# Readback of expert rows: the last four columns summed by TensorE through diagonal gate matrices, with their loads issued second

## The chip, the cores and the metric

One core of one Trainium2 chip (trn2). The metric is the device time of one execution of the whole program in microseconds, here the median of three runs.

## The reference, cut to what matters

The program computes a small two-layer network on 8 images (64 patches each) with 8 texts (128 tokens each), 1536 tokens of 192 features in f32. Layer 0 has a recurrent mixer and a mixture of 8 experts, layer 1 a linear attention and a second mixture of 8 experts. The change lies where the first mixture's result is added to the residual and the attention of layer 1 begins:

```python
# layer 0, experts: each token takes its two best experts
for e in range(8):
    y = gelu(flat_x @ w1[e] + b1[e]) @ w2[e] + b2[e]
    out = out + y * gates[:, e:e + 1]
h = h + out
# layer 1, attention
x = layernorm(h)
qkv = einsum('bnc,dc->bnd', x, qkv_w)
q_, k_ = relu(q) + SCALE, relu(k) + SCALE
kv = einsum('bnhe,bnhd->bhed', k_, v)
out = einsum('bnhe,bhed->bnhd', q_, kv) * z
h = h + out @ proj_w.T + proj_b
```

## The kernel before, in words

The residual h is kept in SBUF as 12 columns of 128 tokens by 192 features (h[:, j, :], j = 0 to 11; columns 0-3 hold the patches, 4-11 one text each). xn and a1 are buffers of the same shape.

Order of the work is written out by hand: each engine has one instruction stream (a block per engine), and semaphores join them.

*The experts of layer 0* work on 28 tiles of 128 token slots. For each tile TensorE writes the products of the second weights, VectorE copies them out of PSUM (L1697) and GpSimd scatters the rows to a DRAM buffer, expert_rows, with an indirect DMA (L797): one row for each token and choice, 1536 rows for the first choice and 1536 for the second. ScalarE copies weights and does the Gelu.

*The readback.* load_acc (lines 560 to 569) waits for all scatters and then loads the rows back in token order: SyncE's queue brings those of the first choice into xn, ScalarE's queue those of the second into a1. Each does so in four loads by the groups of ACC = ((0, 2), (2, 4), (4, 8), (8, 12)): columns 0-1, 2-3, 4-7 and 8-11, in this order, each with a semaphore acc_ld[g] for both queues together. A load of two columns has 192 KB, one of four 384 KB. Behind them SyncE's queue issues 32 loads of the layer-1 expert weights (L631 to L634), and then one copy.

*The sums*, on VectorE (L1754 to L1763): for each group of columns it waits for the group's two loads, then adds gate times row to h, one instruction for each column and choice (L1759, all columns of the first choice, then all of the second). ln_start (L1270, L1273) makes mean and variance of each column of the group. ScalarE takes the root (ln_std, L883), VectorE makes 1/root and the shift (ln_end, L1289 and L1290, two small operations); ScalarE normalizes into xn (ln_norm, L896, one instruction a column). ln_end of a group stands between the first and the second half of the next group's sums; that of the last group stands behind the first k_evac.

*Layer-1 projections.* TensorE transposes pairs of normalized columns (t_pair(3, q), L1985), ScalarE copies them out (xt3_evac, L1181). kv_mms(g) makes keys and values of four columns (L2383, L2389), q_mms(g) the queries (L2415, L2420). VectorE applies relu to keys (k_evac, L1771) and queries (q_evac, L1779), ScalarE copies the values (v_evac, L1190, L1191), behind k_evac. q_mms(0) waits for rwg_ready, since its banks 6 and 7 were used before by filler products and by small products that VectorE copies out (L1751 to L1753). Then come the attention's sums (L2437, L2443, L2459, L2464), the transposes (L2471) and the output projection (L2494).

*Fillers.* keep_busy(n, bank) (L1931) issues n products of 512 columns whose result nobody reads; 18 of them stand before the first transposes of layer 1. Such products also stand ahead of the routing of both layers.

*Table loads.* ScalarE loads a table when its function changes to another set: once after load_acc, for the root (at L883).

Of the kernel before, what the change touches and what calls it, by code (L numbers as in the profile page):

```python
# [30 lines left out]
ACT = mybir.ActivationFunctionType  # L31
# [71 lines left out]
def build(nc, x, out):  # L103
    ctx = ExitStack()
    with ctx:
# [217 lines left out]
        qT = carve(reg2, NK * NTOK)[0:KC, :].rearrange("p (g t) -> p g t", g=NK)  # L323
        kb = carve(reg2, NJ * D).rearrange("p (j n) -> p j n", j=NJ)
# [62 lines left out]
        rank_mm = sem("rank_mm"); oneB_ready = sem("oneB_ready"); lg1_ready = sem("lg1_ready"); one_ready = sem("one_ready")  # L387
# [174 lines left out]
        def load_acc(eng, p):  # L562

            wait_scatters(eng, 0)
            buf = (xn, a1)[p]
            rows = tok_rows(ybuf, p * NTOK)
            for g, ab in enumerate(ACC):
                js = slice(*ab)
                eng.dma_start(buf[:, js, :], rows[:, js, :]).then_inc(acc_ld[g], 16)
# [292 lines left out]
        def _(act):  # L862
# [313 lines left out]

            load_acc(act, 1)
# [17 lines left out]
            for q in range(2):  # L1195
                ln_std(3, q)
                ln_norm(3, q, h)
                xt3_evac(q)
            for g in range(1, 3):
                ln_std(3, g + 1)  # L1200
                ln_norm(3, g + 1, h)
                v_evac(g - 1)
                xt3_evac(2 * g)
                xt3_evac(2 * g + 1)
# [41 lines left out]
        def _(dve):  # L1246
# [507 lines left out]
            for g, ab in enumerate(ACC):  # L1754

                dve.wait_ge(acc_ld[g], 16 * 2)
                for k, y in ((0, xn), (1, a1)):
                    for j in range(*ab):
                        ins = V.scalar_tensor_tensor(out=h[:, j, :], in0=y[:, j, :], scalar=gate[:, k, j:j + 1],  # L1759
                                                     in1=h[:, j, :], op0=ALU.mult, op1=ALU.add)  # L1760
                    link(ins)
                    if g and k == 0:
                        ln_end(3, g - 1)  # L1763
                ln_start(3, g, h)

# [120 lines left out]
            for g in range(2):  # L1886
                k_evac(g)
                if g == 0:
                    ln_end(3, 3)
                q_evac(g)  # L1890
# [33 lines left out]
        def _(pe):  # L1924
# [444 lines left out]
            keep_busy(18, 6)  # L2369
# [31 lines left out]
            def q_mms(g):  # L2401


                if g:
                    pe.wait_ge(q_ev, 2 * g)
                else:

                    pe.wait_ge(rwg_ready, 1)
# [226 lines left out]
```

## Time and profile before

| | |
|---|---|
| median of 3 runs | 430.27 us |
| lowest, highest | 426.57, 430.79 us |
| the profiled execution: device time | 428.35 us |
| its span, first to last instruction | 426.6 us |
| granted TensorE clock, mean over the span | 0.958 |

The profiled execution is one of its own beside the three; 1.75 us of its time lie outside the span. Times in the rows are us from the start of the span. PE is TensorE, DVE VectorE, ACT ScalarE, POOL GpSimd, SP SyncE; a q behind the name is an engine's sequencer or queue. Lines such as L1759 are lines of the kernel before.

### The profile page before, as it was taken

What the parts mean: (1) busy time and instruction counts of PE and PEld (TensorE: products, weight loads), DVE (VectorE), ACT (ScalarE), POOL (GpSimd) and SP (SyncE); (2) the same over time, 40 slices, a digit from 0 to 9 for tenths busy, and PEclk for the clock granted to TensorE, in tenths of its full rate; (3) what the DMA queues carried; (4) which work ended last, traced back from release to release, by engine and by line L of the source; (5) the groups of instructions that cost most, each with busy time, mean ns of one, the idle gap of its engine ahead of it and who ended that gap; (6) DMA issues with size and microseconds to landing.
All of it is one profiled execution on the core that took longest, in us unless ns stands there. A gap on an engine that the chain in (4) does not pass through costs nothing.

```text
span 426.6 us, 11079 instructions
## 1 busy us (share of the span) xinstructions
PE 398.4 (93%) x3904; PEld 299.8 (70%) x3913; DVE 279.8 (66%) x1298; ACT 230.3 (54%) x424; POOL 221.3 (52%) x233
## 2 busy tenths in 40 slices
PE   8999999998769999999788999978999999999993
PEld 5653756666434666666535689538999999999993
DVE  6689999889974444444495368876565656556551
ACT  1287963560675566665146115575565656666550
POOL 5323779798036677774400003444566565566524
PEclk9899689999988999999699999969999999999999
DMA  8609300010142222221499996522243333343323
GB/s 243 112 13 263 73 0 2 2 37 1 34 141 70 60 78 77 84 77 48 131 273 229 233 230 183 171 44 72 46 66 47 67 51 61 47 67 55 47 21 35
DMA packets 38921, 38.29 MB, mean 90 GB/s; under 512 B 7667, under 2 KB 36129, under 8 KB 38853
## 3 DMA queue, kind: packets, MB, share of 16 engines
q1 hardware_dynamic: 27937, 22.85, 22.0%
q0 software_dynamic: 9024, 13.44, 16.4%
q10 hardware_dynamic: 1906, 1.30, 1.0%
q8 instruction: 32, 0.52, 0.5%
q14 instruction: 22, 0.18, 0.1%
HBM read 27.73 MB, written 10.53 MB: 90 GB/s over the span
## 4 chain that ended last, share of the span: by engine, by line
DMA 23%; PE 14%; DVE 5%; issue 5%; ACT 2%; POOL 1%; POOLq 1%; DVEq 0%; ACTq 0%
DMA out<-a,idx 21%; PE bank L2494 2%; PE bank L2095 2%; DVE h L1759 2%; PE bank L2383 1%; PE bank L2140 1%; PE bank L2464 1%; POOL out L809 1%; PE bank L1931 1%; DMA a<-expert_rows 1%; PE bank L2415 1%; DVE st L1270 1%; PE bank L2389 1%; ACT reg L1073 1%; PE bank L2437 1%
## 5 line engine op out<-in xcount | busy, mean ns | idle before, releaser
L809 POOL DMA_INDIRECT out<-a,idx x31 | 50.4, 1626 | 46.6 <-DMA out<-a,idx 32.8
L789 POOL DMA_INDIRECT reg<-xn_rows,idxs x59 | 57.7, 978 | 27.1 <-issue 14.5
L2095 PE MATMUL bank<-reg,xT 64*128 64x128 f32 x1116 | 69.2, 275 | 0.5 <-DVE reg L1671 0.5
L2140 PE MATMUL bank<-reg 64*128 64x192 f32 x744 | 65.6, 323 | 0.0
L2095 PEld LDWEIGHTS bank<-reg,xT 64*128 64x128 f32 x1116 | 65.2, 188 | 0.6 <-DVE reg L1671 0.6
L2140 PEld LDWEIGHTS bank<-reg 64*128 64x128 f32 x744 | 60.0, 187 | 0.0
L1105 ACT ACTIVATE reg<-reg 128x1152 f32 x31 | 36.1, 1163 | 33.8 <-PE bank L2140 33.8
L1700 DVE TENSOR_SCALAR a<-bank,gs 128x192 f32<-128x192 f32 x31 | 13.0, 418 | 53.3 <-PE bank L2140 53.3
L1931 PE MATMUL bank<-con 128*128 128x512 bf16 x154 | 42.4, 429 | 1.5 <-issue 1.0
L797 POOL DMA_INDIRECT expert_rows<-a,idx x28 | 27.6, 985 | 15.4 <-DVE a L1697 9.3
L1697 DVE COPY a<-bank 128x192 f32<-128x192 f32 x28 | 10.0, 358 | 36.2 <-PE bank L2133 36.2
L2078 PE MATMUL bank<-reg,xTs 96*64 (+1 forms) x112 | 33.2, 419 | 0.5 <-DVE xTs L1661 0.5
L2081 PE MATMUL bank<-xT,xTs 96*64 96x288 f32 (+1 forms) x112 | 33.2, 419 | 0.0
L1671 DVE TENSOR_SCALAR reg<-bank,gb 128x128 f32<-128x128 f32 x93 | 32.3, 402 | 0.0
L1931 PEld LDWEIGHTS bank<-con 128*128 128x128 bf16 x163 | 17.2, 110 | 21.1 <-issue 8.3
L2130 PE MATMUL bank<-reg 96*64 x168 | 31.9, 326 | 0.0
L2133 PE MATMUL bank<-xT,reg 96*64 96x192 f32 x168 | 31.9, 326 | 0.0
L1124 ACT ACTIVATE xT<-reg 97x576 f32 x28 | 19.1, 682 | 23.5 <-PE bank L2133 23.5
L838 POOL TENSOR_SCALAR onep<-rs 128x3 f32<-128x3 f32 x4 | 0.9, 230 | 53.4 <-DVE nm L1282 53.4
L2130 PEld LDWEIGHTS bank<-reg 96*64 96x64 f32 x168 | 22.7, 136 | 7.5
L1088 ACT ACTIVATE reg<-bank 128x384 f32<-128x384 f32 x31 | 15.2, 491 | 16.2 <-PE bank L2095 16.2
L2133 PEld LDWEIGHTS bank<-xT,reg 96*64 96x64 f32 x168 | 22.7, 136 | 0.0
(373 smaller groups left out, 878.5 us busy)
## 6 DMA issues: line engine op xcount, KB each, us to landing
reg<-in_w2b SPq DMA_DIRECT2D x8, 576.0 KB, 10.8
reg<-in_w1b SPq DMA_DIRECT2D x8, 288.0 KB, 10.5
reg<-in_w1a SPq DMA_DIRECT2D x8, 216.0 KB
reg<-in_w2a SPq DMA_DIRECT2D x8, 216.0 KB
reg<-in_w1b SPq DMA_DIRECT2D x8, 192.0 KB, 8.4
xn_rows<-xn SPq DMA_DIRECT2D x3, 384.0 KB, 2.6
reg<-in_patchT SPq DMA_DIRECT2D x2, 512.0 KB, 5.5
reg<-xn_rows,idxs POOLq DMA_INDIRECT x59
```

The costliest lines, as they stand in the source:

```text
L789: pool.indirect_dma_start(xs[:, i % RING, 0:(D, D2)[l]], None, xd[l], bass.IndirectOffsetOnAxis(ap=idxs[:, i:i + 1], axis=0)).then_inc(xs_ ...
L797: pool.indirect_dma_start(ybuf, bass.IndirectOffsetOnAxis(ap=idx2[:, i:i + 1], axis=0), ys[:, i % YRING, :], None).then_inc(scat[i % YRING ...
L809: pool.indirect_dma_start(out, bass.IndirectOffsetOnAxis(ap=idx2[:, i:i + 1], axis=0), ys[:, i % YRING, :], None, compute_op=ALU.add).then ...
L1105: nc.scalar.activation(w2r[:, p, :], w2b.rearrange("p e c n -> p (e c n)")[:, bass.ds(e * W2R, W2R)], ACT.Copy).then_inc(w2r_act, 1)
L1671: ins = V.tensor_scalar(dst[:, k], src[:, :, 64 * k:64 * k + 64], gb2[:, 0, k:k + 1], gb2[:, 1, k:k + 1], ALU.mult, ALU.add)
L1931: MM(bank[bk][:, :], con[:, 0:P // 2].bitcast(BF16), con[:, 0:2 * P].bitcast(BF16), start=True, stop=True)
L2078: MM(bank[2 + p][0:GR, 0:hid], xTs[0:r, p, k, 0:GR], w1v[0:r, bass.ds(e * (NK * hid) + k * hid, hid)], start=(k == 0), stop=(k == NK - 1))
L2081: ins = MM(bank[2 + p][GR:P, 0:hid], xTs[0:r, p, k, GR:P], w1u[0:r, i % 3, k * hid:(k + 1) * hid], start=(k == 0), stop=(k == NK - 1))
L2095: ins = MM(bank[2 + 2 * p + a][:, c * P:(c + 1) * P], w1r[rs, p, col:col + hc], xT64[rs, p, k, :], start=(c == 0 and k == 0), stop=(c == n ...
L2130: MM(bank[6 + p][0:GR, 0:D], hTs[0:r, p, c * P:c * P + GR], w2v[0:r, bass.ds(e * (nhc * D) + c * D, D)], start=(c == 0), stop=(c == nhc - 1))
L2133: ins = MM(bank[6 + p][GR:P, 0:D], hTs[0:r, p, c * P + GR:(c + 1) * P], w2u[0:r, i % 2, c * D:(c + 1) * D], start=(c == 0), stop=(c == nhc ...
L2140: ins = MM(bank[Y_BANKS[i == NT - 1][a]][:, 0:D], hT2[rs, p, c * P:(c + 1) * P], w2r[rs, p, c * D:(c + 1) * D], start=(c == 0), stop=(c == ...
```

## The change

What it does:
- load_acc issues its four loads in the order 0, 3, 1, 2: columns 0-1, 8-11, 2-3, 4-7.
- ScalarE, after the last products of the layer-0 experts and ahead of load_acc on its queue, scales the identity by each of the gates of columns 8-11: dg, eight 128x128 diagonal matrices (two choices, four columns), in the space of the layer-0 weights.
- TensorE, after 16 instead of 18 filler products, waits for the loads of columns 8-11, for dg and for rwg_ready, and sums in PSUM, for each of the four columns, identity times h, first diagonal times the first choice's rows, and second diagonal times the second's. That is 12 products of 192 columns, in banks 6 and 7, two columns of tokens in each.
- ScalarE copies the two banks to h (two copies of 128x384), behind the transposed copy of the second pair and ahead of the norm of columns 4-7. q_mms(0) waits for these copies.
- VectorE has no sums of columns 8-11 any more; it waits for the copies and makes mean and variance. ln_end of groups 2 and 3 stands behind that, ahead of the first k_evac. ln_end of groups 0 and 1 moves to the middle of the next group's first half.
- ScalarE's two last roots (groups 2 and 3) stand together ahead of both norms.

```diff
--- before.py
+++ after.py
@@ -321,6 +321,7 @@
         w2a = carve(reg2, NE * (HID0 // HC0) * D)[0:KC + 1, :].rearrange("p (e c n) -> p e c n", e=NE, n=D)
         o = 0
         qT = carve(reg2, NK * NTOK)[0:KC, :].rearrange("p (g t) -> p g t", g=NK)
+        dg = reg2[:, 0:2 * 4 * P].rearrange("p (k j n) -> p k j n", k=TOPK, j=4)
         kb = carve(reg2, NJ * D).rearrange("p (j n) -> p j n", j=NJ)
         vb = carve(reg2, NJ * NK * KV).rearrange("p (j n) -> p j n", n=KV)
         vb4 = vb.rearrange("p (j a) n -> p j a n", a=NK)
@@ -384,7 +385,7 @@
         back_mm = sem("back_mm")
         xd_written = sem("xd_written")
         sums_mm = sem("sums_mm"); rsum_ready = sem("rsum_ready"); h_added = sem("h_added"); lg_mm = sem("lg_mm"); ex_in = sem("ex_in"); ex_out = sem("ex_out"); msk_ready = sem("msk_ready")
-        rank_mm = sem("rank_mm"); oneB_ready = sem("oneB_ready"); lg1_ready = sem("lg1_ready"); one_ready = sem("one_ready")
+        rank_mm = sem("rank_mm"); oneB_ready = sem("oneB_ready"); dg_ready = sem("dg_ready"); add_mm = sem("add_mm"); add_ev = sem("add_ev"); lg1_ready = sem("lg1_ready"); one_ready = sem("one_ready")
         gate_ready = sem("gate_ready")
         slot_ready = sem("slot_ready"); oneP_ready = sem("oneP_ready"); oneS_ready = sem("oneS_ready")
         inv_mm = sem("inv_mm")
@@ -564,8 +565,8 @@
             wait_scatters(eng, 0)
             buf = (xn, a1)[p]
             rows = tok_rows(ybuf, p * NTOK)
-            for g, ab in enumerate(ACC):
-                js = slice(*ab)
+            for g in (0, 3, 1, 2):
+                js = slice(*ACC[g])
                 eng.dma_start(buf[:, js, :], rows[:, js, :]).then_inc(acc_ld[g], 16)
 
 
@@ -1174,6 +1175,11 @@
             experts(0, ACT.Gelu, HID0)
 
 
+            act.wait_ge(g2_mm, NT0)
+            for k in range(TOPK):
+                for n, j in enumerate(range(*ACC[3])):
+                    nc.scalar.activation(dg[:, k, n, :], con[:, C_ID:C_ID + P], ACT.Identity,
+                                         scale=gate[:, k, j:j + 1]).then_inc(dg_ready, 1)
             load_acc(act, 1)
             def xt3_evac(q):
 
@@ -1196,8 +1202,14 @@
                 ln_std(3, q)
                 ln_norm(3, q, h)
                 xt3_evac(q)
+            act.wait_ge(add_mm, 1)
+            for b in range(2):
+                nc.scalar.activation(h[:, 8 + 2 * b:10 + 2 * b, :],
+                                     bank[6 + b][:, 0:2 * D].rearrange("p (j n) -> p j n", j=2),
+                                     ACT.Copy).then_inc(add_ev, 1)
+            ln_std(3, 2)
+            ln_std(3, 3)
             for g in range(1, 3):
-                ln_std(3, g + 1)
                 ln_norm(3, g + 1, h)
                 v_evac(g - 1)
                 xt3_evac(2 * g)
@@ -1751,17 +1763,21 @@
             V.tensor_copy(rsum[:, :, :], bank[7][:, 0:2 * NE].rearrange("p (v e) -> p v e", v=2))
             V.tensor_copy(prw[0:KC, :, D:DL], bank[7][0:KC, 3 * NE:5 * NE].rearrange("p (m e) -> p m e", m=NK))
             V.tensor_copy(prw[KC:KC + 1, 1, D:DL], bank[7][KC:KC + 1, 2 * NE:3 * NE]).then_inc(rwg_ready, 1)
-            for g, ab in enumerate(ACC):
+            for g, ab in enumerate(ACC[0:3]):
 
                 dve.wait_ge(acc_ld[g], 16 * 2)
                 for k, y in ((0, xn), (1, a1)):
-                    for j in range(*ab):
+                    for n, j in enumerate(range(*ab)):
                         ins = V.scalar_tensor_tensor(out=h[:, j, :], in0=y[:, j, :], scalar=gate[:, k, j:j + 1],
                                                      in1=h[:, j, :], op0=ALU.mult, op1=ALU.add)
+                        if g and k == 0 and n == (ab[1] - ab[0]) // 2 - 1:
+                            ln_end(3, g - 1)
                     link(ins)
-                    if g and k == 0:
-                        ln_end(3, g - 1)
                 ln_start(3, g, h)
+            dve.wait_ge(add_ev, 2)
+            ln_start(3, 3, h)
+            ln_end(3, 2)
+            ln_end(3, 3)
 
             def k_evac(g):
 
@@ -1885,8 +1901,6 @@
 
             for g in range(2):
                 k_evac(g)
-                if g == 0:
-                    ln_end(3, 3)
                 q_evac(g)
             state(0)
             k_evac(2)
@@ -2366,7 +2380,17 @@
                              start=(k == 0), stop=(k == NK - 1))
             ins.then_inc(bias_mm, 1)
 
-            keep_busy(18, 6)
+            keep_busy(16, 6)
+            pe.wait_ge(acc_ld[3], 16 * 2)
+            pe.wait_ge(dg_ready, TOPK * 4)
+            pe.wait_ge(rwg_ready, 1)
+            for n, j in enumerate(range(*ACC[3])):
+
+                rows_j = bank[6 + n // 2][:, (n % 2) * D:(n % 2 + 1) * D]
+                MM(rows_j, ident, h[:, j, :], start=(n % 2 == 0), stop=False)
+                MM(rows_j, dg[:, 0, n, :], xn[:, j, :], start=False, stop=False)
+                ins = MM(rows_j, dg[:, 1, n, :], a1[:, j, :], start=False, stop=(n % 2 == 1))
+            ins.then_inc(add_mm, 1)
             t_pair(3, 0)
 
             def kv_mms(g):
@@ -2405,7 +2429,7 @@
                     pe.wait_ge(q_ev, 2 * g)
                 else:
 
-                    pe.wait_ge(rwg_ready, 1)
+                    pe.wait_ge(add_ev, 2)
 
                 def half(m):
                     return slice(m * 2 * P, (m + 1) * 2 * P)
```

## Rows read from the trace of the kernel before

**Rows 1.** Part 1 of the page: busy us, share of the span, instructions, by engine.
```profile
PE 398.4 (93%) x3904; PEld 299.8 (70%) x3913; DVE 279.8 (66%) x1298; ACT 230.3 (54%) x424; POOL 221.3 (52%) x233
```

**Rows 2.** Chain that ended last, 195 to 262 us: start us, us, what.
```profile
205.30 2.35 DMA expert_rows<-a,idx
...
207.87 4.00 DMA a<-expert_rows
...
214.36 0.64 DVE h L1759 x2
...
216.98 0.79 DVE h L1759 x3
...
218.67 1.33 DVE h L1759 x4
...
221.57 0.39 DVE h L1759 x2
...
224.62 1.15 DVE st L1270 x4
...
226.20 0.57 DVE reg L1771
...
228.35 1.55 PE bank L2383 x4
...
252.13 2.24 PE bank L2494 x12
```

**Rows 3.** Third and fourth load of a queue: issues (start, us), us to landing.
```profile
210.19 1.13 ACTq L569 DMA_DIRECT2D a<-expert_rows  x2
...
a<-expert_rows ACTq DMA_DIRECT2D x1, 384.0 KB, 5.2
xn<-expert_rows SPq DMA_DIRECT2D x1, 384.0 KB, 5.9
...
210.76 0.56 ACTq L569 DMA_DIRECT2D a<-expert_rows  x1
...
xn<-expert_rows SPq DMA_DIRECT2D x1, 384.0 KB, 8.0
a<-expert_rows ACTq DMA_DIRECT2D x1, 384.0 KB, 10.2
```

**Rows 4.** Timeline around the readback, and L1073: start us, us, engine line, [idle before].
```profile
204.00 0.32 PE L2133 MATMUL bank<-xT,reg 97*64 97x192 f32 x1
...
210.55 5.09 PE L1931 MATMUL bank<-con 128*128 128x512 bf16 x17 [0.23 <-issue]
...
211.35 1.28 ACT L883 ACT_TABLE_LOAD   x1 [8.61 <-issue]
...
218.70 0.98 ACT L896 ACTIVATE xn<-h,nmr,rstd 128x192 f32<-128x192 f32 x2 [0.99 <-DVE nmr L1290]
...
223.30 1.86 ACT L896 ACTIVATE xn<-h,nmr,rstd 128x192 f32<-128x192 f32 x4 [1.40 <-DVE nmr L1290]
...
223.45 1.97 PE L2415 MATMUL bank<-reg 128*96 128x256 f32 x8
...
226.39 0.87 PE L1985 MATMUL bank<-con,xn 128*128 128x128 f32 x6
...
227.71 0.88 ACT L1181 ACTIVATE reg<-bank 128x384 f32<-128x384 f32 x2
...
278.37 1.57 ACT L1073 ACTIVATE reg<-iotab,slf 128x128 f16<-128x128 f16 x5 [3.38 <-DVE slf L1591]
```

**Rows 5.** TensorE after two gaps: timeline, and windows (us, busy, PEclk, DMA).
```profile
117.61 0.46 PE L2011 MATMUL bank<-msk,con 128*128 128x96 f32 x2 [2.02 <-DVE msk L1546]
...
206.31 1.02 PE L2360 MATMUL bank<-rwg,con 96*128 96x8 f32 x4 [1.98 <-DVE reg L1746]
...
206.30:213.10 6.80, 6.56 (x26) 0.50 0.56 151
...
117.60:121.00 3.40, 3.39 (x19) 1.00 0.86 257
```


## The prediction

> **What bounds the kernel now.** I read the page first: TensorE is busy for 398.4 of 426.6 us and no other engine for more than 280 [rows 1]. That is a mean over stages, so the next view was the chain of waits around the readback, the stage that the change touches. In it the reader is to see three limits one after the other [rows 2]. The last scatter of expert rows lands at 205.30 + 2.35 = 207.65. Then a load decides: issued at 207.87, landed 4.00 later, at 211.87, for the first two columns. From there VectorE decides: the sums of columns 2-3 start at 214.36, of 4-7 at 216.98, of 8-11 at 221.57, and the relu of the keys, L1771, at 226.20. TensorE takes over at 228.35 with the second group of key and value products, and from there to past 250 the chain is TensorE alone. So the figure that carries to the end is the 228.35: what moves it moves the end by as much, and what doesn't is worth nothing.
>
> The third view was the landings, since VectorE looks bound by its own work only as long as its data are there first [rows 3]. The third load of each queue (columns 4-7) starts at 210.19 and takes 5.2 on ScalarE's queue and 5.9 on SyncE's, which started within 0.02 us of it: 216.1 for both. The fourth (8-11) starts near 210.7 and takes 8.0 on SyncE's queue, 218.7, and 10.2 on ScalarE's, 210.76 + 10.2 = 220.96. VectorE asked for them at 216.98 and 221.57: 0.9 and 0.6 us of slack. The loads are nearly as late as the sums. That is the number of this case.
>
> **The change, part by part.** The sum goes against the profiled execution: span 426.6, 428.35 us in all, 1.9 below the median of the three runs (430.27). What I find as a difference I add to the median.
>
> *Sums taken off VectorE.* Eight multiply-adds go. Four take 1.33 us [rows 2], so 2.7 us. The statistics of columns 8-11 stay (224.62 to 226.20, 1.58 us). The two small operations of ln_end(3,3), which ran between two evacuations, now come before them. Their price: 226.20 - 221.57 = 4.63 is eight multiply-adds (2.67), the statistics (1.58) and one ln_end, so 0.37 for that. If nothing is waited for, VectorE is 2.3 us sooner at L1771.
>
> *Order of the loads.* The bytes and the number of issues are the same, the order is columns 0-1, 8-11, 2-3, 4-7 on both queues, with the 32 weight loads behind them on SyncE's queue as before. I take the landings by columns moved: 2 by 211.87, 8 by 216.1, 12 by 220.96 (an estimate from [rows 2, 3], as nothing is issued more or sooner). So columns 8-11 land at some 214.7 (six columns, in line between the first two), 2-3 at 216.1, and 4-7 at 220.96. VectorE is free for 2-3 at 214.36 and waits 1.7 us. Its work on them is 216.98 - 214.36 = 2.62, so it asks for 4-7 at 218.7 and waits 2.2 us more. Bounds for this last landing, which I call L: 216.98 or sooner (no wait, below) and 220.96 plus what ScalarE adds, next. SyncE's 218.7 lies between them. I take 220.96, since the sum needs both queues and ScalarE's was the later.
>
> *Diagonal matrices on ScalarE.* Eight scalings of 128x128 wait for the last product of the experts (204.00 + 0.32) and stand ahead of load_acc on that queue. ScalarE was idle from 211.35 - 8.61 = 202.74 [rows 4], so the loads are what they could delay. Five operations of the same width with a pointer operand took 1.57, 0.31 each; four of 192 columns took 1.86, 0.47 each [rows 4]. Eight are 2.5 to 3.7 us, ending at 206.9 to 208.1 against the scatter's 207.65. I take the 0.31 of equal width: hidden, 0.7 us to spare. The other end costs 0.45, and a table load, 1.28 [rows 4], would cost up to 1.7 in all; I keep that as the top of the range of L.
>
> *Products on TensorE.* Two of 18 filler products go (17 recorded ones take 5.09 us to 215.64, 0.3 each [rows 4]), so the filler ends near 215.1. Then it waits for the load of 8-11 (214.7), for dg_ready and rwg_ready (both long there). Twelve products of 96x200 took 2.24 [rows 2]; twelve of 192 columns over all 128 rows I take at 2.2. Bounds: twelve times half of a 392-column product (1.55 / 4 / 2) is 2.3, and one alone without overlap is no more than a whole such product, 4.7 for twelve. Queued behind them on TensorE are the transposes of columns 0-1. These need their norms: landing 216.1, one sum (0.33), ln_end (0.37), two norms (0.98), 217.9. The products end at 217.3: hidden, by the wait for columns 2-3; at 4.7 they would end at 219.8 and hold the first transposes 1.9 us, but these are then still ahead of the next ones at L + 2.1. Without that wait (norms at 216.1) they would stand 1.3 us in the way of the first transposes, but not of VectorE.
>
> *Copies out of PSUM on ScalarE.* Two of 128x384, 0.49 each by its like at 227.71 (0.88 for two overlapped) [rows 4]. They come after the norm of 2-3 and its copy, L + 3.2, and end at L + 4.2. VectorE reaches them after its group of four columns, 221.57 - 216.98 = 4.59, at L + 4.6: hidden with 0.4 us to spare. The new wait of the query products for them costs nothing either, as those start at L + 5.8 (next).
>
> *Scalings amid the sums.* ln_end after half of the first half of a group instead of after all of it: 0.33 us sooner for a pair, 0.67 for four. It is used above. It gains nothing where a load is late.
>
> **The sum from L to the hand-over.** Sums and statistics of 4-7: 4.59. Statistics of 8-11: 1.58. ln_end(3,2): 0.37. Four norms on ScalarE: 1.86 and 0.04 to start. They used to be done at 225.2 (223.30 + 1.86) [rows 4], before L1771; now they come after it and in front of the value copies. That eats what VectorE gave. Value copies: 227.71 - (226.20 + 0.57) = 0.94. First xT3 copy to the first product of the second group: 228.35 - 227.71 = 0.64. In all L + 10.0. TensorE's own way there: two sums and ln_end 1.04, two norms 1.02, then as before 223.45 - (218.70 + 0.98) = 3.77 to the query products and 226.39 - 223.45 = 2.94 to the next transposes: L + 8.8, later than the norms (L + 8.4) but within what the value copies take.
> With L = 220.96 the hand-over is at 231.0 against 228.35: +2.6 us. It is even at L = 218.3. **Forecast: 430.27 + 2.6 = 432.9 us**, some 431.0 for an execution like the profiled one. All behind runs on TensorE, shifted.
>
> **Rivals.** *A, the loads land ahead of need; not slower.* With columns 2-3 by 214.36 and 4-7 by 216.98 the hand-over is 216.98 + 10.0 = 227.0, -1.4: 428.9. One place decides, L, and the point is 218.3. For it: the third issue starts only at 210.19, 2.3 after the first; if the queues ran short of work behind that, a second load of four columns in place of two would fill the gap. SyncE's own last landing was 218.7, only 0.4 over. Against it: the same bytes have to pass before L, and ScalarE's queue needed to 220.96.
> *B, TensorE's clock falls in the new wait.* The first transposes start at 217.9, take some 0.44 (half of the six at 226.39), their copy 0.5, the first key products 1.55: TensorE then idles from 220.4 to L + 2.1 = 223.1, 2.7 us. Before, it idled 1.98 us up to 206.31, and the granted clock from there to 213.10 was 0.50, the 1.2 GHz level [rows 5]. But it also idled 2.02 us up to 117.61, and the clock behind that stayed at 1.00, the 2.4 GHz level [rows 5]: such a gap can bring a fall, and need not. From 223.1 some 6.6 us of products lie ahead of the hand-over. With a fall there that lasts as long as that one, 6.8 us, 3.4 are done by 230.1 and the rest by 233.4, the hand-over comes near 234.1, +5.7: 436.0. The Trainium skill (TensorE: Matmul & The Clock Gate, "HAM oscillation") says that a kernel whose bursts of products are parted by waits on DMA is throttled again and again and begins its bursts cold. By that rule B is the outcome; the gap before 117.61 speaks against its certainty.
> *C, ScalarE's scalings hold up its loads.* With 0.47 each or a table load L moves by 0.45 to 1.7: +3.1 to +4.3, 433.4 to 434.6. One engine's queue decides, and the table load would be seen before 207.
> *D, nothing reaches the hand-over:* L near 218.3, loads and sums even, 430.3.
>
> **How the numbers follow.** Forecast 0.46, A 0.16, B 0.19, C 0.06, D 0.13. The three runs shown lie 4.2 us apart, so a change under 1% (4.3 us) is about what this kernel can't tell from none. Faster by over 1% needs under 426.0, three times A's gain: 0.06. Slower needs over 434.6, which is B, the upper part of C and the forecast in a bad draw: 0.24. The rest is 0.70. The range: down to 427.5, A with a lucky draw of runs; up to 436.5, B.
>
> **What would show it.** Right: VectorE idle before the first L1759 of column 2 (some 1.7 us) and of column 4 (some 2), both put down to a load; the second L2383 group near 231; L896 for 4-7 after L1771; the twelve products done before the transposes of 0-1; no table load before the readback. If the clock row between 220 and 230 shows 0.50, it is B. If VectorE waits for nothing there, or the fourth load lands before 218.3, the forecast is wrong and A or D holds. If the scalings end after 207.7, it is C. A change of the end that isn't the change of the hand-over would mean that a stage behind it, not this one, moved.

## The result, and the profile after

| | before | changed |
|---|---|---|
| median (20 runs each) | 427.62 us | 429.74 us |
| lowest, highest | 425.54, 430.79 | 426.71, 432.35 |
| ratio, 95% interval | | 1.0056 (1.0037 to 1.0076) |
| profiled execution: time, span | 428.35, 426.6 us | 426.71, 424.9 us |

By the ratio the change costs 0.56%, 2.4 us (1.6 to 3.2); the two medians lie 2.1 us apart. The forecast was 2.6 us slower. Its absolute 432.9 lay 3.2 us too high, and 2.65 of these are the median of three on which it stood (430.27, against 427.62 for twenty).

The profiled execution of the changed kernel is the fastest of its twenty, and its span is shorter than that of the profile before: its readback alone starts 2.83 us sooner in the span. So absolute times of the two profiles can't be compared. I compare from t0, the start of the first load of the readback (before 207.87, ScalarE's queue), to the hand-over, the first product of the second key group, which is L2383 before and L2407 after.

The chain of waits of the changed kernel, 204 to 232 us (start us, us, what), where every piece from the filler on is one of TensorE's or a copy that it waits for:

```profile
206.20 6.28 PE bank L1945 x16
212.48 0.33 PE bank L2390 x2
...
216.06 0.33 PE bank L2392 x2
216.38 0.34 PE bank L1999 x3
...
216.75 0.50 ACT reg L1187
...
226.12 0.50 ACT reg L1187
...
226.75 1.55 PE bank L2407 x4
```

Its t0 is 205.04 and the hand-over 226.75: t0 + 21.71, against 228.35 - 207.87 = 20.48 in [rows 2]. That is 1.2 us later. Where VectorE's sums stood in the chain before, there now stands TensorE: sixteen fillers, twelve products (L2390 to L2392), the first transposes, ScalarE's copy of them (216.75), TensorE's own work up to the next transposes, and their copy (226.12).

The products by form, from the groups of instructions between 203 and 230 us (count, busy us, mean ns of one record, idle before):

```profile
L2390 PE MATMUL bank<-h,con 128*128 128x192 f32 x8 | 2.0, 326 | 0.0
L2391 PE MATMUL bank<-xn,reg 128*128 128x192 f32 x8 | 2.0, 326 | 0.0
L2392 PE MATMUL bank<-a,reg 128*128 128x192 f32 x8 | 2.0, 326 | 0.0
```

They are twelve matrix products in the code and 24 records in the trace: each f32 product leaves two, of 0.326 us each and overlapping by half. The chain above has a product ("x2") every 0.33 us: 12 x 0.33 = 3.9 us, from 212.48 to 216.38.

The landings, from the DMA view in narrow windows (SyncE's third issue begins at 206.31, the fourth of ScalarE's at 206.95), answering [rows 3]:

```profile
xn<-expert_rows SPq DMA_DIRECT2D x1, 384.0 KB, 5.0
a<-expert_rows ACTq DMA_DIRECT2D x1, 384.0 KB, 5.5
...
a<-expert_rows ACTq DMA_DIRECT2D x1, 192.0 KB, 5.6
xn<-expert_rows SPq DMA_DIRECT2D x1, 192.0 KB, 6.1
...
xn<-expert_rows SPq DMA_DIRECT2D x1, 384.0 KB, 8.1
a<-expert_rows ACTq DMA_DIRECT2D x1, 384.0 KB, 9.1
```

Behind t0: columns 8-11 by 6.0, 2-3 by 7.4, 4-7 by 11.0. The last landing of the readback came at t0 + 13.1 before.

The timeline of the same stretch (start us, us, engine, line, idle before and its releaser), which answers [rows 4]; L1771 is the L1759 of before, L1787 its L1771, L897 its L896, L1187 its L1181, and the L1181 of this view is the line of ScalarE's scalings:

```profile
203.62 0.38 ACT L1181 ACTIVATE reg<-con,gate 128x128 f32<-128x128 f32 x1
...
207.47 1.28 ACT L884 ACT_TABLE_LOAD   x1 [3.47 <-issue]
...
212.43 0.42 DVE L1771 SCALAR_TENSOR_TENSOR h<-xn,gate,h 128x192 f32<-128x192 f32 x1 [1.43 <-DMA xn<-expert_rows]
...
216.04 0.75 DVE L1771 SCALAR_TENSOR_TENSOR h<-xn,gate,h 128x192 f32<-128x192 f32 x2 [0.87 <-DMA a<-expert_rows]
...
216.75 0.49 ACT L1187 ACTIVATE reg<-bank 128x384 f32<-128x384 f32 x1 [2.61 <-PE bank L1999]
...
217.46 0.17 DVE L1301 RECIPROCAL rstd<-std 128x2 f32<-128x2 f32 x1 [0.67 <-ACT std L884]
...
223.71 1.02 DVE L1787 TENSOR_SCALAR reg<-bank 128x384 f32<-128x384 f32 x2
```

VectorE waits for columns 2-3 (1.43) and for 4-7 (0.87), and a third time, 0.67 us for the root of columns 2-3 at 217.46. The mean and variance for that root were there at 215.17, but ScalarE stood in its own order at the copy of the first transposes (2.61 idle at 216.75), and these came late because TensorE was at its products. No table load comes before the scalings; the only one of the readback follows the loads, as before.

### The profile page after: what moved, and what is told of

It is laid out like the page before. It is cut to its first block, busy times and chain, and to the rows that moved or that the text cites. A ratio compares the mean times of both kernels' runs of the same rounds, so it can differ in the third digit from the quotient of the medians.

```text
span 424.9 us, 11132 instructions
## 1 busy us (share of the span) xinstructions
PE 400.2 (94%) x3935; PEld 300.3 (71%) x3935; DVE 277.1 (65%) x1290; ACT 233.4 (55%) x434; POOL 221.4 (52%) x233
## 4 chain that ended last, share of the span: by engine, by line
PE 49%; DMA 25%; DVE 10%; ACT 6%; issue 6%; POOL 3%; POOLq 1%; DVEq 0%; ACTq 0%
DMA out<-a,idx 24%; PE bank L2092 7%; PE bank L2144 6%; PE bank L1945 3%; PE bank L2201 3%; PE bank L2407 2%; PE bank L2518 2%; DVE bank L1421 2%; PE bank L2271 2%; PE bank L2067 2%; ACT reg L1074 1%; PE bank L1960 1%; PE bank L2439 1%; PE bank L1953 1%; PE bank L2313 1%
## 5 line engine op out<-in xcount | busy, mean ns | idle before, releaser
L790 POOL DMA_INDIRECT reg<-xn_rows,idxs x59 | 57.7, 978 | 26.5 <-issue 14.3
L1945 PE MATMUL bank<-con 128*128 128x512 bf16 x161 | 43.6, 426 | 0.0
L798 POOL DMA_INDIRECT expert_rows<-a,idx x28 | 27.6, 986 | 14.3 <-DVE a L1709 8.2
## 6 DMA issues: line engine op xcount, KB each, us to landing
reg<-in_w1b SPq DMA_DIRECT2D x8, 288.0 KB, 11.3
```

Of the source, the lines that this page charges most:

```text
L790: pool.indirect_dma_start(xs[:, i % RING, 0:(D, D2)[l]], None, xd[l], bass.IndirectOffsetOnAxis(ap=idxs[:, i:i + 1], axis=0)).then_inc(xs_ ...
L798: pool.indirect_dma_start(ybuf, bass.IndirectOffsetOnAxis(ap=idx2[:, i:i + 1], axis=0), ys[:, i % YRING, :], None).then_inc(scat[i % YRING ...
L1945: MM(bank[bk][:, :], con[:, 0:P // 2].bitcast(BF16), con[:, 0:2 * P].bitcast(BF16), start=True, stop=True)
```

## The experiments

One table first, since all profiles are read by the same figures: us behind t0, from the timeline, chain and DMA view of each profile. L, here and below, is the landing of columns 4-7. Landings are good to 0.1 us. "Tail" is from the hand-over to the end of the span.

| profile | columns 2-3 | 4-7 | last landing | products end | hand-over | tail |
|---|---|---|---|---|---|---|
| before | 5.8 | 8.3 | 13.1 | | 20.48 | 198.2 |
| changed | 7.4 | 11.0 | 11.0 | 11.3 | 21.71 | 198.2 |
| changed_again | 8.8 | 12.8 | 12.8 | 11.8 | 22.81 | 197.9 |
| loads_alone | 9.4 | 13.5 | 13.5 | | 25.03 | 199.6 |
| products_alone | 6.0 | 8.4 | 12.8 | 11.2 | 22.42 | 199.7 |
| norm_first | 9.0 | 12.9 | 12.9 | 12.0 | 22.84 | 199.6 |
| fewer_fillers | 10.1 | 14.6 | 14.6 | 14.3 | 24.67 | 198.1 |
| hold_weights | 9.0 | 11.0 | 11.0 | 12.0 | 22.35 | 199.6 |
| hold_weights_before | 6.1 | 8.5 | 10.7 | | 20.19 | 198.2 |
| keys_first | 6.0 | 9.6 | 13.7 | | 20.39 | 199.4 |
| keys_first_again | 5.7 | 9.6 | 13.4 | | 20.32 | 198.1 |
| keys_first_held | 6.4 | 8.7 | 11.0 | | 19.77 | 199.4 |
| products_sooner | 7.9 | 10.1 | 10.1 | 10.5 | 21.64 | 198.1 |

### loads_alone: only the order of the loads

```diff
-            for g, ab in enumerate(ACC):
-                js = slice(*ab)
+            for g in (0, 3, 1, 2):
+                js = slice(*ACC[g])
```

> The kernel before with only the order of the readback's loads changed (0, 3, 1, 2); VectorE still sums all four groups in the order 0, 1, 2, 3. t0 is the start of the first load. Theory Loads (the late landing of columns 4-7 decides): VectorE waits for columns 2-3 and again for 4-7, which land 11 to 13 us behind t0, and reaches the first relu of the keys 9.2 us behind that landing, at t0 + 20.2 to 22.3 against t0 + 18.3 before: 1.9 to 4.0 us slower. Theory Array (what the change costs is TensorE's products, the loads are nearly free): under 0.7 us slower.

431.66 us against 427.26: ratio 1.0088 (1.0054 to 1.0122), 3.8 us. Its chain, 204 to 235 us, and below it two lines of VectorE's timeline:

```profile
209.48 11.03 DMA a<-expert_rows
...
229.88 0.57 DVE reg L1771
```

```profile
216.45 0.75 DVE L1759 SCALAR_TENSOR_TENSOR h<-xn,gate,h 128x192 f32<-128x192 f32 x2 [3.43 <-DMA xn<-expert_rows]
...
220.54 1.41 DVE L1759 SCALAR_TENSOR_TENSOR h<-xn,gate,h 128x192 f32<-128x192 f32 x4 [1.35 <-DMA a<-expert_rows]
```

The load that begins at 209.48 needs 11.03 us; VectorE idles 3.43 us for columns 2-3 and 1.35 for 4-7, then runs without a gap to L1771 at t0 + 22.88. The order of the loads alone costs VectorE 4.6 us. L1771 comes at L + 9.4, about as expected (9.2), and later than t0 + 22.3 because L was 13.5 and not 11 to 13. Array's "under 0.7 us" lies outside the interval (2.3 to 5.2 us) and is out for this part.

One thing more happened here. TensorE stood 3.86 us in front of its first transposes, and its granted clock was 0.50, the 1.2 GHz level, from 219.3 to 222.7:

```profile
219.40:222.70 3.30, 2.91 (x4) 1.17 (x4) 2.09 (x8) 0.85 (x3) 0.00 (x0) 0.50 1.11 233
```

That is what rival B describes. It did not reach the hand-over, since the chain from the landing on is VectorE's.

### products_alone: only the scalings and the products

```diff
+            act.wait_ge(g2_mm, NT0)
+            for k in range(TOPK):
+                for n, j in enumerate(range(*ACC[3])):
+                    nc.scalar.activation(dg[:, k, n, :], con[:, C_ID:C_ID + P], ACT.Identity,
+                                         scale=gate[:, k, j:j + 1]).then_inc(dg_ready, 1)
             load_acc(act, 1)
...
-            keep_busy(18, 6)
+            keep_busy(16, 6)
+            pe.wait_ge(dg_ready, TOPK * 4)
+            pe.wait_ge(rwg_ready, 1)
+            for n in range(4):
+                rows_j = bank[6 + n // 2][:, (n % 2) * D:(n % 2 + 1) * D]
+                MM(rows_j, ident, con[:, 0:D], start=(n % 2 == 0), stop=False)
+                MM(rows_j, dg[:, 0, n, :], con[:, 0:D], start=False, stop=False)
+                MM(rows_j, dg[:, 1, n, :], con[:, 0:D], start=False, stop=(n % 2 == 1))
```

> The kernel before with only the eight scalings on ScalarE ahead of its loads, 16 instead of 18 fillers, and twelve products of the change's shapes behind them, on constant data that is there already; nobody reads them, and VectorE still does all sums. Theory Loads: the products are hidden by the wait for the norms or nearly, 0 to 0.3 us slower. Theory Array: they take 3.9 us (0.325 for each of 24 records), the first transposes come 2.5 us later, ScalarE's copy behind them holds the root of columns 2-3, and VectorE waits for it in front of its second half of columns 4-7: about 2 us slower.

429.84 us against 427.26: ratio 1.0059 (1.0036 to 1.0083), 2.5 us. Array holds here, with its size (about 2 us expected, 1.5 to 3.5 measured). The timeline of 210 to 222 us:

```profile
216.18 0.49 PE L1991 MATMUL bank<-con,xn 128*128 128x128 f32 x3
216.70 0.49 ACT L1187 ACTIVATE reg<-bank 128x384 f32<-128x384 f32 x1 [3.34 <-PE bank L1991]
...
217.48 0.17 DVE L1295 RECIPROCAL rstd<-std 128x2 f32<-128x2 f32 x1 [2.25 <-ACT std L884]
```

Nothing reads these products. Still VectorE stands 2.25 us between the halves of columns 4-7, for a root; ScalarE, which takes it, stood 3.34 us for the first transposes; and they stood behind the products. My forecast had called this "hidden".

### fewer_fillers: 12 instead of 16 ahead of the products

```diff
-            keep_busy(16, 6)
+            keep_busy(12, 6)
```

> The changed kernel with 12 instead of 16 fillers ahead of the products. Theory Loads: TensorE is not what is waited for, no change against the changed kernel, so 2.1 us slower than before. Theory Array: the products start up to 1.5 us sooner, as soon as columns 8-11 are there, the first transposes too, and the hand-over to TensorE comes 0.7 us sooner than in the changed kernel: 1.2 to 1.5 us slower than before. A fall of the clock behind the shorter run of fillers could take it back.

430.61 us against 427.26: ratio 1.0090 (1.0056 to 1.0124), 3.8 us. Neither number came. The profile shows two things at once. Its loads landed later than in any other profile (columns 8-11 at t0 + 8.4, 4-7 at t0 + 14.6), which the fillers don't explain; and the clock fell in the middle of the products. Its chain, and a row of the windows view (us, busy by engine, PEclk, DMA):

```profile
207.74 7.91 DMA a<-expert_rows
...
216.61 0.33 PE bank L2392 x2
216.93 0.63 PE bank L2390 x2
217.56 0.64 PE bank L2391 x2
...
231.91 1.55 PE bank L2407 x4
```

```profile
216.80:220.20 3.40, 3.40 (x12) 3.40 (x11) 2.60 (x10) 0.98 (x2) 0.00 (x0) 0.50 1.10 247
```

With fewer fillers TensorE stood 1.9 us in front of the products, for the load of columns 8-11, and from 216.81 on they ran at 0.64 instead of 0.33 a product, at the 1.2 GHz level, for 3.4 us. That is rival B again, and it cost some 1.7 us of products. The chain here goes by these products and not by L: they end at t0 + 14.3, and the hand-over is that + 10.4. But L, at 14.6, would have put it at the same place (L + 10.06), so the fall of the clock cost this execution next to nothing. As a test of Array it is inconclusive.

### norm_first: norms and first relu ahead of the last statistics

```diff
-            dve.wait_ge(add_ev, 2)
-            ln_start(3, 3, h)
             ln_end(3, 2)
-            ln_end(3, 3)
...
             for g in range(2):
                 k_evac(g)
+                if g == 0:
+                    dve.wait_ge(add_ev, 2)
+                    ln_start(3, 3, h)
+                    ln_end(3, 3)
                 q_evac(g)
```

(ScalarE takes the two last roots each ahead of its own norm.)

> The changed kernel with VectorE's order behind the sums of columns 4-7 turned: ln_end of these, the first relu of the keys, and only then the wait for the copies and the statistics of columns 8-11; ScalarE takes the two last roots apart again. Theory Loads (the chain behind the landing L of columns 4-7 is VectorE's and ScalarE's, L + 10.7 as measured): it shortens to about L + 9, 1.1 us or more off the changed kernel's time, so 1 us slower than before or less. Theory Array (TensorE's own way, L + 9.5 to the end of the query products, is just behind): 0.2 to 0.4 us off the changed kernel's time.

430.90 us against 427.26: ratio 1.0097 (1.0062 to 1.0133), 4.1 us, no gain at all; both numbers expected are missed. Its timeline, 216 to 229 us:

```profile
223.53 1.86 ACT L897 ACTIVATE xn<-h,nmr,rstd 128x192 f32<-128x192 f32 x4 [0.44 <-DVE nmr L1301]
...
227.37 0.87 ACT L1187 ACTIVATE reg<-bank 128x384 f32<-128x384 f32 x2 [1.08 <-PE bank L1999]
```

The norms of 4-7 start at L + 5.5 here; in changed_again they start at L + 6.5. Yet the hand-over is L + 10.0 in both (22.84 - 12.86, 22.81 - 12.84): ScalarE then stands 1.08 us at 227.37 for TensorE's transposes. So the chain behind L is TensorE's own from the second transposes on, L + 2.1. Why the time came out even above the changed kernel's (its interval overlaps that one's only from 1.0062 to 1.0076) stays open; the hand-over of this one profile is that of changed_again.

### changed_again: the changed kernel once more

> The changed kernel once more, for a second profile of it: its first had the last landing 11.0 us behind the start of the loads (t0), while the kernel before and four others had 12.8 to 14.6. Theory Loads: the last landing L is 12.8 or later here and the hand-over to TensorE (second group of key products) comes at L + 10 to 10.8, that is t0 + 23 to 24, against 20.5 before and 21.7 in the first profile; the time is 2 to 3 us above before. Theory Array: the hand-over does not follow L but stays at t0 + 21.7.

430.05 us against 427.92: ratio 1.0051 (1.0028 to 1.0074). The chain of this second profile:

```profile
208.82 10.40 DMA a<-expert_rows
...
219.24 0.75 DVE h L1771 x2
...
220.30 0.99 ACT xn L897 x2
...
221.33 0.55 PE bank L1999 x3
...
228.05 0.49 PE bank L1999 x3
...
229.19 1.55 PE bank L2407 x4
```

Here the fourth load decides. It lands at 219.22, t0 + 12.84; two sums, ln_end and two norms follow, and TensorE takes over at L + 2.1. The hand-over is 229.19 = L + 9.97. The forecast's sum from L, 10.0, is met to 0.03. Loads holds: the hand-over followed L, by 0.2 us less than the t0 + 23 at the lower end of what was expected.

### hold_weights: the weight loads only behind the readback

```diff
             load_acc(sp, 0)
+            sp.wait_ge(acc_ld[2], 16 * 2)
```

> The changed kernel with one wait more: SyncE issues the 32 loads of layer-1 weights only when columns 4-7 have landed, so the readback has the DMA engines to itself. Theory Loads (their landing decides, and the weights slow it): L comes down to 9.5 to 10.5 us behind t0, the hand-over to some t0 + 21, and the time to 0.5 us above before or less. Theory Array (the products and what queues behind them decide): the hand-over stays where the products put it, t0 + 21.7, the time 1.2 us or more above before.

428.72 us against 427.92: ratio 1.0022 (0.9999 to 1.0045). That lies between the two theories (0.5 us or less, 1.2 or more). By the middle values more than half of the cost is gone; the interval overlaps those of changed and changed_again, so it is likely and not certain. Its chain:

```profile
205.15 7.27 DMA a<-expert_rows
...
212.47 0.59 PE bank L2391 x2
...
216.64 0.34 PE bank L2000 x3
...
227.01 1.55 PE bank L2408 x4
```

L is down to 11.0 and no longer in the chain; what is there is the second load (columns 8-11, 7.27 us), then the products to 216.6, and TensorE to the hand-over at 227.01. So there are two limits, and the later one counts: landing of 4-7 + 10.0, and end of the products + 10.4 (21.71 - 11.35 in the first profile of the changed kernel, 22.35 - 11.98 here). In the kernel before neither stood as late. The hand-over of this one profile, 22.35, is 1.9 above before, while the time is only 0.9 us above: columns 8-11 landed as late as 7.8 here (6.0 and 7.6 in the two profiles of the changed kernel), and one profile doesn't give the mean of the runs.

### hold_weights_before: the same wait in the kernel before

The edit is that of hold_weights with acc_ld[3].

> The kernel before with the same wait, for columns 8-11, ahead of the weight loads. Theory Loads: before the change the loads were 0.6 us ahead of VectorE's sums, so an earlier landing gives nothing, 0 to -0.4 us. If the weights come too late for the experts of layer 1, it is slower; they had some 20 us to spare.

427.10 us against 427.92: ratio 0.9992 (0.9964 to 1.0019), as expected no difference. The last landing is 2.4 us sooner and nobody waits for it.

### keys_first, keys_first_again: the first relu ahead of the last sums

The sums of a group became a function, and in the kernel before:

```diff
-            for g, ab in enumerate(ACC):
...
+            for g in range(3):
+                group(g)
+            ln_end(3, 2)
...
                 k_evac(g)
                 if g == 0:
+                    group(3)
                     ln_end(3, 3)
```

> The kernel before, sums all on VectorE and loads in the old order, with the first relu of the keys (and ln_end of columns 4-7) ahead of the sums of columns 8-11 instead of behind them. By the view that VectorE's chain sets the hand-over, and TensorE's own way ends at t0 + 19.5 (transposes of columns 4-5 at 18.5 + 0.44, copy 0.5): the hand-over comes 0.8 to 1.0 us sooner, and the time is 0.8 us below before. If something behind it (norms of columns 8-11, needed for the transposes at t0 + 25) is late instead, no gain.

426.90 us against 427.92: ratio 0.9976 (0.9950 to 1.0002), 1.0 us below by the middle value.

> keys_first once more, since its interval (0.9950 to 1.0002) just held no change and keys_first_held showed none. If the hand-over, 0.1 us sooner in the profile of keys_first and 0.7 in that of keys_first_held, reaches the end: 0.5 to 0.9 us below before, a ratio of 0.998 to 0.999. Rival: the clock's low stretch at the routing of layer 1, 6.8 us in one piece in some profiles and 10.2 in one or two pieces in others, gives it back at random: a ratio within 0.1% of 1.

427.58 us against 427.18: ratio 1.0013 (0.9987 to 1.0039). Between them they show no gain that could be told from none. In both profiles VectorE waited for columns 4-7 (0.9 and 1.1 us), so the hand-over was at 20.39 and 20.32: what VectorE gave, the loads took.

### keys_first_held: both together

> keys_first and hold_weights_before together: sums all on VectorE in the old order of loads, the first relu of the keys ahead of the sums of columns 8-11, and the weight loads issued only when the readback has landed. In the profile of keys_first columns 4-7 landed 9.6 us behind t0 and VectorE waited 0.9 us for them. Theory (max of two limits: landing of 4-7, and TensorE's own way): without the weights they land by t0 + 8.4, the hand-over comes at t0 + 19.3 to 19.6 against 20.5 before, and the time is 0.9 us below before. Rival: the gain given back behind the hand-over, no difference.

427.74 us against 427.60: ratio 0.9994 (0.9969 to 1.0018). The hand-over came at t0 + 19.77, 0.7 sooner than before and 0.2 later than expected. The time doesn't show it, and can't exclude it either: 0.7 us is 0.17%, inside the interval. In the one profile the tail, 199.4 instead of 198.2 (last section), takes more than that back. No version of this study beats the kernel before by more than the noise.

### loads_alone_held: the order alone, weights held

The edits of loads_alone and hold_weights.

> loads_alone with the weight loads issued only when columns 4-7 have landed. Theory Loads: hand-over = L + 11.5 as in loads_alone (25.0 - 13.5), and L comes down to 11 or to VectorE's own need (landing of columns 2-3, near 9, + 2.6): hand-over at t0 + 22.5 to 23.2 instead of 25.0, the time 2 us above before instead of 3.8. Rival: the weights' share of the DMA engines is not what makes the last landing late: 25, 3.8 us.

431.46 us against 427.60: ratio 1.0082 (1.0053 to 1.0111), 3.5 us, by the time the rival's number. The landing did come sooner, t0 + 11.3. The profile is of an execution of 442.75 us, far above the others. A piece of its chain and a row of the windows view show why its hand-over, t0 + 24.20, says little:

```profile
230.22 2.98 PE bank L2384 x4
```

```profile
227.60:234.20 6.60, 4.89 (x12) 2.78 (x14) 6.39 (x27) 2.97 (x7) 0.00 (x0) 0.50 0.64 157
```

TensorE stood 5.35 us in front of its first transposes, the clock was at the 1.2 GHz level from 227.5 to 234.3, and two key products took 2.98 us instead of 1.58. So here, unlike in loads_alone, TensorE's own way set the hand-over. VectorE, whose four sums take 1.40 us here as in loads_alone, reached the first relu (L1772) at 238.48, t0 + 21.28, 1.6 us sooner than in loads_alone. The loads did give VectorE what the theory says; that the time of the other executions shows no more than 0.3 us of it stays open. A fall of the clock in most of them would explain it, and no profile shows that.

### products_sooner: columns 8-11 loaded first, weights held, 12 fillers

```diff
-            for g in (0, 3, 1, 2):
+            for g in (3, 0, 1, 2):
...
-            keep_busy(16, 6)
+            keep_busy(12, 6)
```

> hold_weights with columns 8-11 loaded first of all and 12 instead of 16 fillers. There the hand-over was the end of the products (t0 + 12.0) + 10.4. Theory (products' end + 10.4, or landing of 4-7 + 10.0, the later): the products start at t0 + 6 and end at t0 + 10, the hand-over comes at t0 + 21 to 21.5, 1 us sooner than in hold_weights, if the landing of 4-7 stays at 11 or sooner; time no more than 0.5 us above before. Rival: the shorter run of fillers or the longer wait lets the clock fall and takes it back; 2 us above before.

429.43 us against 427.60: ratio 1.0059 (1.0032 to 1.0086). The products ran from t0 + 6.4 to 10.5, but the hand-over was 21.64, only 0.7 sooner than in hold_weights, and 0.8 behind the products' end + 10.4. Its chain:

```profile
205.39 6.03 DMA a<-expert_rows
...
211.44 0.76 DVE h L1772 x2
...
217.62 0.99 ACT xn L898 x2
...
218.66 0.55 PE bank L2000 x3
```

Columns 0-1 now land at t0 + 6.5. From there VectorE works without a gap to the norms of columns 2-3, and the second transposes wait for these. That is a third limit, VectorE's sums from the first landing on, which the theory of two limits left out. The time, 2.5 us above before, is that of the rival, though the clock did not fall behind the products in this profile; the tail was of the short kind. What the time is made of beyond the hand-over's 1.2 us is open.

## Why the prediction was right or wrong

**The direction: right. The mechanism: right in one of the two profiles of the changed kernel.** VectorE idles for columns 2-3 and for 4-7 in both (1.43 and 0.87; 2.53 and 1.29). loads_alone shows the reorder by itself: 3.8 us. What VectorE lost by it is larger than the 2.7 us that it was relieved of. But only changed_again has the fourth load in its chain. In the first profile there is no load in it, and the hand-over is set by the products, which the forecast had put at nothing ("hidden").

**The difference: 2.6 forecast, 2.4 measured (1.6 to 3.2), 2.2 on the repeat.** That they are so close is in part luck. Two errors of the sum have opposite signs: L was taken at 13.1, and came at 11.0 and 12.8; the products were taken at 2.2 us and in nobody's way, and are 3.9 and set a limit of their own. The hand-overs of the two profiles are 1.2 and 2.3 us later than before, not 2.6.

**The level: wrong**, 432.9 against 429.74. Two steps failed. The one that cost most of the number is the first paragraph of "the change, part by part", "What I find as a difference I add to the median": that was the median of three, 430.27, and twenty executions give 427.62. The profiled 428.35, which I had beside it, was nearer. The one in the mechanism is the term "Products on TensorE": 2.2 us, hidden, where the runs show 3.9 us, an end at t0 + 11.3 to 11.8, and from there 10.4 us to the hand-over.

**Point by point.**
- *L = 220.96, t0 + 13.1.* 11.0 in the first profile, 12.8 in the second, 12.9 and 14.6 in norm_first and fewer_fillers. The estimate by columns moved holds in two of these four; its t0 + 8.2 for columns 2-3 was met by 7.4 to 10.1. One number was taken where there is a spread of 3.6 us.
- *The products, 2.2 us.* The term that was mis-sized. Measured 3.9. I priced them by "Twelve products of 96x200 took 2.24 [rows 2]", but the row's x12 counts records, and an f32 product leaves two: those were six products. The lower bound of 2.3 has the same error in it: the row's 1.55 for x4 is two products of 392 columns, so half of one is 0.39 and not 0.19. The upper bound of 4.7 held them, by luck of the same double count.
- *"Hidden, by the wait for columns 2-3", and at the upper end "still ahead of the next ones".* Failed. It looked at TensorE's queue only. Behind the first transposes ScalarE's copy stands in front of the root of 2-3, and VectorE waits for it in the middle of 4-7. products_alone: 2.25 us at that place, 2.5 us in the end. In the first profile of the changed kernel it is 0.67, and none in changed_again, where L is so late that the root is there.
- *From L to the hand-over, 10.0.* Met where L decides (9.97 in changed_again, 9.98 in norm_first). But not by the path that I added up. I took norms and value copies; norm_first moved the norms 1.0 us ahead and the hand-over stayed at L + 10.0. The path is TensorE's: L + 8.8 to the transposes, as I had it, and 0.5 + 0.5 + 0.14 to the first product. Two ways of equal length, and I named the wrong one.
- *The scalings, hidden.* Right: the last begins at 203.62, takes 0.38 and ends 1.0 us before the first load starts (205.04). No table load. Rival C is out.
- *Copies, and ln_end in the middle of a half.* Right for the copies: VectorE goes from the statistics of 4-7 to those of 8-11 without a gap. The new place of ln_end has the 0.67 us wait of the first profile.
- *VectorE 2.3 us sooner at L1771 without waits.* It was t0 + 18.67 and 19.77 instead of 18.33.
- *Rival B, the clock.* It did not happen in either profile of the changed kernel, and the gap that was to bring it was hardly there: TensorE stood 0.0 and 0.6 us in front of the second transposes instead of 2.7, as the late products filled it. In three other profiles the clock did fall behind a wait of TensorE for a load, or for work that stood behind a load: 1.89 us of idling in fewer_fillers, 3.86 in loads_alone, 5.35 in loads_alone_held. changed_again had 1.90 us of idling in front of its products, and its clock stayed at 1.00 from there to 232. So such a gap can bring a fall and need not, as the forecast had it. The Trainium skill's remark (TensorE: Matmul & The Clock Gate, "HAM oscillation") on bursts parted by waits on DMA is borne out by those three profiles, and not as a certainty. B's 6.8 us at half speed were to be over "by 230.1"; 223.1 + 6.8 is 229.9, and nothing hangs on the 0.2.
- *Rival A.* It did not come. Its point, L = 218.3, is t0 + 10.4, and the earliest L of the changed kernel is t0 + 11.0. With that L the sum gives a hand-over at t0 + 21.0, 0.5 later than before; the products made it 21.71. So A's -1.4 couldn't have come: with no wait for any load, end of products + 10.4 is still above 20.5.

**What it is made of.** In the execution with L = 12.8 the loads decide, in that with L = 11.0 the products, 1.1 us apart. Which of the two decides in how many of the twenty executions, two profiles can't tell. hold_weights takes the last landing out of the decision in its profile, and by the middle values 0.2% remains of 0.5%. The parts are not additive (3.8 and 2.5 alone, 2.4 together). That they stand in parallel and that VectorE is relieved would explain it; no run takes these two apart.

## What to carry to other kernels

Before work is moved from one engine to another, look at how much time its data had to spare: here the loads were 0.6 us ahead of the sums, so an engine made faster by 2.7 us could only wait. Follow each delayed instruction through the in-order queue of every engine that touches its result, not only that of its own. And count instructions in the code, not records in the trace: for f32 products there are twice as many, and a row's "x12" is six products.

## What the runs showed of the hardware that I had not expected

**Landings spread.** The same 2.3 MB over the same two queues, last landing 10.1 to 14.6 us behind t0. The later weight loads take a part: with them held it was 10.1 to 11.3 in five profiles, beside them 11.0 to 14.6 in nine. The part of ScalarE's queue is the one that is late: SyncE's last was at 9.8 to 10.9 in all of the profiles that had the weights behind it.

**The end of the program comes in two lengths.** From the hand-over to the end of the span it is 197.9 to 198.2 us in seven profiles and 199.4 to 199.7 in six (loads_alone_held left out), whatever the kernel. In all of the seven the clock at the routing of layer 1 (from 280 on) is at 0.50 for one stretch of 6.8 us; in the six it falls for 3.4 us twice, with 3.4 between, or stays low for 10.2 us. keys_first has the long end and keys_first_again, the same kernel, the short one. The windows view of the kernel before and of keys_first_held, 288.5 to 290.5 us (busy by engine, then PEclk):

```profile
288.50:290.50 2.00, 1.03 (x16) 0.90 (x18) 1.93 (x9) 0.00 (x0) 1.36 (x2) 1.00 0.37 93
```

```profile
288.50:290.50 2.00, 2.00 (x22) 2.00 (x22) 1.23 (x5) 0.00 (x0) 1.27 (x2) 0.50 0.45 120
```

At that place the second ran at 1.2 GHz what the first ran at 2.4. The difference arises there. ScalarE's copy of 128x384 behind that routing starts at 292.19 in the kernel before and at 292.36 in keys_first, after waits of unlike length for TensorE:

```profile
292.19 0.49 ACT L1088 ACTIVATE reg<-bank 128x384 f32<-128x384 f32 x1 [3.81 <-PE bank L2095]
292.36 0.49 ACT L1088 ACTIVATE reg<-bank 128x384 f32<-128x384 f32 x1 [5.04 <-PE bank L2101]
```

And from its scalings in front of the routing (281.6 in the kernel before) to the end it is 144.7 to 145.0 us in the seven and 146.2 to 146.4 in the six, while from a copy at 298.6 to the end it is 127.9 to 128.0 in all. So some 1.4 us of a run are a matter of which pattern it draws, more than what most changes here move, and a single profile's end can't judge a change of this size. The hand-over behind t0 is free of that draw, though not of the draw of the landings.
